# Later source numbers, a later loop for far rows and earlier block offsets in a two-layer graph kernel on one Trainium2 core

## The chip, the core and the metric

The kernel runs on one core of one Trainium2 chip. The core has five engines with a queue of instructions each: PE (TensorE, matrix products), DVE (VectorE), ACT (ScalarE), POOL (GpSimd, which here issues the indirect gathers) and SP (SyncE, which issues most other DMAs). They meet only at semaphores. The metric is the device time of one execution in microseconds (us); the lower, the better.

## The reference, cut to what matters

Two graph layers follow each other on 6250 nodes of 128 features and 100000 edges. The edges are sorted by `dst`. `src` is in no order.

```
msg = h[src] + sum_over_heads(leaky_relu(attn[rel] * (e @ fc_w.T)))     # layer 0
x   = layernorm(x + segment_sum(msg, dst))
h   = x @ W.T + b                                                       # layer 1
s1, s2 = h @ a1_w + a1_b, h @ a2_w + a2_b
e   = leaky_relu(s1[src] + s2[dst])
ex  = exp(e - segment_max(e, src)[src])
out = segment_sum((ex / segment_sum(ex, src)[src])[:, None] * h[dst], src)
x   = layernorm(x + out)
```

## The kernel before, in words

**Layer 0** is a counted loop over 196 groups of 512 edges. It also writes each edge's record (destination and place of its source within a block) into a table in DRAM (`table`, shown as `sorted_edges`) at its place in the order of the sources, so that layer 1 can go through the edges block by block. A block is 122 nodes; there are 52 blocks.

**The passage between the layers.** Thirteen chunks of four blocks (`for c in range(HCHUNKS)`) are turned on PE (L1072), normalised, and multiplied by W (L1077). DVE makes the moments (L1466, L1476) and writes the rows of h (L1471, L1480, counted by semaphore `n_hb`). Each finished chunk goes to DRAM (`h_rows`) in two DMAs: 112 partitions from SP (L543, semaphore `h_out`), 10 partitions from POOL (L659, `h_small`). The sorted records come back as two tables `tab[:, 0]` and `tab[:, 1]`, of which each place is filled in one only, so that their sum is the record. After chunk 4 DVE adds them (L1484, `tab_sum`, semaphore `t_sum`), PE turns the sum into the PSUM banks EP and AP (L1082, `t_turned`), ACT casts it (L830, L831, `t_cast`), and DVE makes from the untransposed sum `loc_i`, `loc_m` and `loc_b` (L1486 to L1488, `s_loc`): the source numbers by row. SP writes `loc_b` to `sorted_sources` in DRAM (L547) and some of `loc_i` to `near_records` (L549, `near_out`) between chunks 6 and 7. After the chunks DVE takes the two fields of the turned records apart: `sd`, the number of the row to gather (L1490, `s_dec`), and `ss` (L1491), which L1494 copies to `ssf`. Then come the scores (L1496 to L1506, `l1_ready`) and the preparation of "near" and "far" rows (L1510 to L1537), which ends with `s_trips`.

**Layer 1** has 208 steps, one for a group of 512 edges of one block. POOL gathers four times 128 rows of `h_rows` per group (`group1`, L671; `late_group1`, L679), three times where the group is "near" (every second one from the ninth on); the fourth part is then made on PE from the blocks that are in SBUF (`near_gather`, L1140) and a row of `far_rows`. There are eight buffers for groups. `group1(g)` for g of 8 or more waits for `step_done` of g - 3, which counts PE's steps. The loop for far rows runs `n_trips` times, which is once for these inputs: ACT picks the row numbers (L908), POOL gathers them (L690), SP writes them to `far_rows` (L560) and waits until that has landed. In SP's program this loop stands ahead of the loads of the source numbers of groups 4 and later (`sources`, L538); the first four are loaded ahead of it. DVE waits for these loads in `members(g + 2)` (L1544), which is a part of its step g.

DVE's step g (`step1`) is written out by hand: `update(g - 5)` (L1549 to L1554: it loads the block's offset from `blk_i` into a register, waits, and adds the sums of PE to that block), the maximum (L1587), some fifteen small operations, `members` (L1544), `spread` (L1629), and in turns `near_shift` (L1638) or `near_add` (L1646). In the last 48 steps (`TAIL`) each step ends with `early`, which finishes one block that no group will touch again: L1688 to L1703, with a wait of DVE for itself between L1702 and L1703. In the last five of them DVE also writes the final form of some blocks (`normal`, L1706).

Of the kernel before, what the change touches and what calls it, by code (L numbers as in the profile page):

```python
# [5 lines left out]
ALU = mybir.AluOpType  # L6
# [25 lines left out]
HC = 4  # L32
# [46 lines left out]
def build(nc, x, x_t, e, src_pg, dst_pg, dst_g, rel_g, fcT, attn, WT, Wn, b, a1, a1b, a2, a2b, out):  # L79
    with ExitStack() as ctx:  # L80
# [394 lines left out]
        def _(sp):  # L475
# [65 lines left out]
            for c in range(HCHUNKS):  # L541
# [3 lines left out]
                if c == HCHUNKS // 2:  # L545
                    sp.wait_ge(s_loc, 1)
                    sp.dma_start(loc_dram.rearrange("g (u r) -> (g u) r", r=P).rearrange("(c p) r -> p c r", p=P),  # L547
                                 loc_b.rearrange("p (c r) -> p c r", r=P)).then_inc(loc_out, 16)
                    sp.dma_start(near_dram.rearrange("(c a) r -> a c r", c=CH),  # L549
                                 loc_i[NEAR_PER * TG - 1:P:NEAR_PER * TG, :].rearrange("p (c r) -> p c r", r=P)).then_inc(near_out, 16)  # L550
            sp.wait_ge(loc_out, 16)
            sp.wait_ge(near_out, 16)
            for k in range(RSLOTS):
                sources(k, k, True)

# [41 lines left out]
            sp.wait_ge(h_out, 16 * HCHUNKS)  # L597
            sp.wait_ge(h_small, 16 * HCHUNKS)
# [11 lines left out]
        def _(pool):  # L610
# [46 lines left out]
            for c in range(HCHUNKS):  # L657
# [3 lines left out]
            pool.wait_ge(h_out, 16 * HCHUNKS)  # L661
            pool.wait_ge(h_small, 16 * HCHUNKS)
# [19 lines left out]
            more = group_count(pool)  # L682
            for k in range(S1):
                group1(k, k, True)
                if k == 1:
# [146 lines left out]

# [129 lines left out]
        def _(pe):  # L962
# [104 lines left out]
            for c in range(HCHUNKS):  # L1067
# [11 lines left out]
                if c == HCHUNKS // 2 - 2:  # L1079
                    pe.wait_ge(t_sum, 1)  # L1080
                    for u in range(CH):
                        mm = pe.transpose((EPS_T, AP_)[u // 4][:, u % 4 * P:(u % 4 + 1) * P],  # L1082
                                          tab_sum[:, u * P:(u + 1) * P], ident[:, :])
                    mm.then_inc(t_turned, 1)
# [87 lines left out]
        def _(dve):  # L1172
# [281 lines left out]
            for c in range(HCHUNKS + 1):  # L1454
# [27 lines left out]
                if c == HCHUNKS // 2 - 2:  # L1482
                    dve.wait_ge(s_srt, 32)
                    v.tensor_tensor(tab_sum, tab[:, 0, :], tab[:, 1, :], ALU.add).then_inc(t_sum, 1)  # L1484
                    dve.wait_ge(t_sum, 1)
                    link(v.tensor_copy(loc_i, tab_sum))  # L1486
                    link(v.tensor_scalar(loc_m, loc_i, 255, P - 1, ALU.bitwise_and, ALU.bitwise_xor))
                    v.tensor_copy(loc_b, loc_m).then_inc(s_loc, 1)  # L1488
# [319 lines left out]
```

## Time and profile before

| | |
|---|---|
| time, median of 3 runs | 2537.67 us (2537.1 to 2540.32) |
| the profiled execution: its own time | 2536.95 us |
| its span in the trace | 2535.1 us |
| busy in the span: PE, DVE, ACT, POOL | 86%, 91%, 77%, 72% |
| mean granted TensorE clock | 0.937 |
| layer 0 ends, layer 1 begins (start of the chunks, first gather) | 1496.98 us, 1541.25 us |

The span runs from the first to the last instruction of the trace; all places in the trace are given in us from its start. Busy shares are means over stages that have different limits.

### The profile page before, as it was taken

The page shows a single profiled execution, that of the slowest core. Times are in us where ns is not written, and L with a number is a line of the kernel's source. Part 1 is how long each engine was busy: PE and PEld are TensorE (multiplying, and loading weights), DVE is VectorE, ACT ScalarE, POOL GpSimd, SP SyncE. Part 2 cuts the span into 40 slices and gives each one's busy share as a digit, 9 for nine tenths or more (in the row PEclk, how much of TensorE's full clock was granted, in tenths as well). Part 3 has the DMA queues.
Part 4 walks back from the last instruction along what each step waited for, and adds up shares of the span by engine and source line. Part 5 has one row for each costly group of instructions (what it writes and reads, how often), then busy time and mean ns, then how long its engine had stood idle before and what let it go on. Part 6 is the DMA issues. An engine that isn't in the chain of part 4 may idle for free. (4 is left out here: it accounts for less than half of the span.)

```text
span 2535.1 us, 49366 instructions
## 1 busy us (share of the span) xinstructions
PE 2173.4 (86%) x12265; PEld 1562.1 (62%) x12266; DVE 2299.6 (91%) x5975; ACT 1950.8 (77%) x5574; POOL 1824.8 (72%) x1746
## 2 busy tenths in 40 slices
PE   6999999999999999999999974766667777777674
PEld 3566666666666666666666654766667666776664
DVE  9999999999999999999999986778887778888886
ACT  5788888888888888888888854777777777776666
POOL 3477777777777777777777745777777777776662
PEclk8999999999999999999999986899998888888886
DMA  4233333333333333333333324444444444443332
GB/s 139 73 101 104 104 106 101 104 103 104 105 106 102 103 103 104 105 106 101 104 102 105 105 58 98 99 100 100 98 101 99 99 100 101 98 99 86 84 82 71
DMA packets 180816, 250.92 MB, mean 99 GB/s; under 512 B 41103, under 2 KB 110172, under 8 KB 180416
## 3 DMA queue, kind: packets, MB, share of 16 engines
q1 hardware_dynamic: 125088, 145.72, 20.2%
q0 software_dynamic: 55456, 102.13, 17.1%
q8 instruction: 103, 1.69, 0.3%
q14 instruction: 169, 1.38, 0.2%
HBM read 238.37 MB, written 9.31 MB: 98 GB/s over the span
## 5 line engine op out<-in xcount | busy, mean ns | idle before, releaser
L627 POOL DMA_INDIRECT room<-in_x,pk x784 | 925.2, 1180 | 262.5 <-issue 252.5
L1010 PE MATMUL FP<-fc_sb,room 128*128 128x512 f32 x1568 | 832.4, 612 | 2.2 <-issue 2.2
L1019 PE MATMUL WP<-at_p,rel_oh 100*128 100x512 f32 x1568 | 804.2, 594 | 0.0
L671 POOL DMA_INDIRECT room<-h_rows,y x666 | 628.9, 944 | 220.5 <-issue 184.9
L754 ACT ACTIVATE w_sb<-WP 128x512 f32<-128x512 f32 x784 | 464.1, 592 | 224.9 <-PE WP L1019 219.5
L1019 PEld LDWEIGHTS WP<-at_p,rel_oh 100*128 100x128 f32 x1568 | 297.9, 190 | 376.4 <-issue 376.4
L1108 PE MATMUL FP<-ident,room 128*128 128x128 f32 x1664 | 278.2, 319 | 277.3 <-DMA room<-h_rows,y 213.9
L1359 DVE TENSOR_TENSOR z<-FP,w_sb 128x1024 f32<-128x1024 f32 x392 | 478.8, 1221 | 1.5 <-ACT w_sb L754 1.0
L1366 DVE SCALAR_TENSOR_TENSOR y<-z 128x2048 f32<-128x2048 f32 x196 | 452.2, 2307 | 0.0
L1108 PEld LDWEIGHTS FP<-ident,room 128*128 128x128 f32 x1664 | 238.0, 220 | 312.9 <-DMA room<-h_rows,y 246.0
L1010 PEld LDWEIGHTS FP<-fc_sb,room 128*128 128x128 f32 x1568 | 266.6, 190 | 43.3 <-issue 2.6
L871 ACT ACTIVATE room<-room,pr 128x129 f32<-128x129 f32 x832 | 266.6, 392 | 6.8
L852 ACT ACTIVATE accT<-accT,neg_big 128x512 f32<-128x512 bf16 x208 | 148.7, 715 | 150.6 <-DVE accT L1544 150.4
L638 POOL DMA_INDIRECT sorted_edges<-runs,spot_i x196 | 185.8, 948 | 90.4 <-issue 60.4
L761 ACT ACTIVATE boh<-arena,rank_pay 128x52 f32<-128x52 bf16 x784 | 239.7, 378 | 0.0
L1374 DVE TENSOR_TENSOR hs<-y 128x1024 f32<-128x1024 f32 x196 | 238.4, 1216 | 0.0
L1029 PEld LDWEIGHTS AP<-doh,room 128*128 128x128 f32 x1568 | 190.6, 192 | 53.5 <-DVE room L1390 53.5
L1029 PE MATMUL AP<-doh,room 128*128 128x64 f32 x1568 | 211.1, 278 | 7.1 <-DVE accT L1350 4.2
L771 ACT ACTIVATE dot<-iota_row,dloc 128x64 bf16<-128x64 f32 x784 | 206.3, 337 | 0.0
L884 ACT ACTIVATE w_sb<-boh 122x640 f32<-122x640 bf16 x100 | 73.6, 736 | 111.3 <-PE WP L1140 108.4
L878 ACT ACTIVATE boh<-w_sb,accT 122x128 bf16<-122x128 int32 x500 | 155.4, 386 | 0.0
L1587 DVE CUSTOM_DVE_ANT_0 hs<-accT,FP 128x512 f32<-128x512 f32 x208 | 142.0, 682 | 12.5 <-issue 6.0
(280 smaller groups left out, 3475.5 us busy)
## 6 DMA issues: line engine op xcount, KB each, us to landing
room<-in_e SPq DMA_DIRECT2D x196, 256.0 KB
rel_sb<-in_rel_g SPq DMA_DIRECT2D x196, 200.0 KB
z<-sorted_sources SPq DMA_DIRECT2D x208, 128.0 KB
room<-in_x,pk POOLq DMA_INDIRECT x784
room<-h_rows,y POOLq DMA_INDIRECT x666
w_sb<-far_rows SPq DMA_DIRECT2D x100, 65.0 KB
w_sb<-near_records SPq DMA_DIRECT2D x101, 61.0 KB
sorted_edges<-runs,spot_i POOLq DMA_INDIRECT x196, 2.0
```

The costliest lines, as they stand in the source:

```text
L627: pool.indirect_dma_start(xg[:, k, u, 0:P], None, x[:, :], bass.IndirectOffsetOnAxis(ap=pk[:, g, u:u + 1], axis=0)).then_inc(xg_in[k], 16)
L671: pool.indirect_dma_start(hg[k][:, u, :], None, h_dram[:, :], bass.IndirectOffsetOnAxis(ap=sd[:, g * TG + u:g * TG + u + 1], axis=0)).then ...
L754: nc.scalar.activation(w_sb[:, u // 2, u % 2, :], WP[u % 2][:, :], ACT.Copy).then_inc(w_copied, 1)
L761: ins = nc.scalar.activation(boh[:, k % 2, u, :], onehot[:, :, bass.ds(g * TG + u, 1)].rearrange("p b o -> p (b o)"), ACT.Identity, bias=0 ...
L871: nc.scalar.activation(hg[k][:, u, 0:P + 1], hg[k][:, u, 0:P + 1], ACT.Identity, bias=0.0, scale=pr[:, k % 2, u:u + 1]).then_inc(h_scaled, 1)
L1010: mm = pe.matmul(FP[u // 2][:, u % 2, :], e_sb[:, k, u, :], fc_sb[:, :], start=True, stop=True)
L1019: mm = pe.matmul(WP[u % 2][:, :], rel_oh[:, k % 2, u * P:(u + 1) * P], at_p[:, j, :], start=(j == 0), stop=(j == 1))
L1029: pe.matmul(AP_[:, 0:W], msg[:, k % 2, u, :], doh[:, k % 2, u, :], start=(u == 0), stop=False)
L1108: mm = pe.matmul(rows_of(k)[:, u * P:(u + 1) * P], hg[k][:, u, P + 1:P + 2].to_broadcast([P, P]), ident[:, :], start=True, stop=True)
L1359: v.tensor_tensor(z[:, h, :, :], FP[h][:, :, :], w_sb[:, h, :, :], ALU.mult).then_inc(z_done, 1)
L1366: v.scalar_tensor_tensor(y[:, :, :, :], z[:, :, :, :], SLOPE0, z[:, :, :, :], ALU.mult, ALU.max).then_inc(y_done, 1)
L1374: v.tensor_tensor(hs[:, :, :], y_all[:, :, 0:D4 // 2], y_all[:, :, D4 // 2:D4], ALU.add).then_inc(hs_done, 1)
```

## The change

The sum of the two tables moves behind the last chunk on DVE. PE no longer waits for it: it forms the turned sum itself, by two products with the identity that add up in PSUM, 16 matmuls in place of 8 transposes. The DMAs of the source numbers and of the near records move behind all chunks on SP, and the copy to `ssf` moves behind the scores on DVE. The last chunk's 10 partitions are written by a DMA of ACT. POOL reads the number of groups ahead of the chunks, and its part of the loop for far rows moves from behind the second group's gathers to behind the sixth's. In the last 48 steps DVE loads the next block offset right behind `spread`, and the last four offsets ahead of the last five updates.

```diff
@@ sync
                              h_sb[0:PMAIN, HC * c:HC * (c + 1), 0:HROW]).then_inc(h_out, 16)
-                if c == HCHUNKS // 2:
-                    sp.wait_ge(s_loc, 1)
-                    sp.dma_start(loc_dram.rearrange("g (u r) -> (g u) r", r=P).rearrange("(c p) r -> p c r", p=P),
-                                 loc_b.rearrange("p (c r) -> p c r", r=P)).then_inc(loc_out, 16)
...
+            sp.wait_ge(s_loc, 1)
+            sp.dma_start(loc_dram.rearrange("g (u r) -> (g u) r", r=P).rearrange("(c p) r -> p c r", p=P),
+                         loc_b.rearrange("p (c r) -> p c r", r=P)).then_inc(loc_out, 16)
+            sp.dma_start(near_dram.rearrange("(c a) r -> a c r", c=CH),
...
             sp.wait_ge(loc_out, 16)
-            sp.wait_ge(near_out, 16)
             for k in range(RSLOTS):
                 sources(k, k, True)
+            sp.wait_ge(near_out, 16)
@@ gpsimd
             pool.memset(o_all, 0.0).then_inc(o_zero, 1)
-            for c in range(HCHUNKS):
+            more = group_count(pool)
+            for c in range(HCHUNKS - 1):
                 pool.wait_ge(n_hb, HC * (c + 1))
...
-            pool.wait_ge(h_out, 16 * HCHUNKS)
-            pool.wait_ge(h_small, 16 * HCHUNKS)
+            pool.wait_ge(h_out, 16 * (HCHUNKS + 1))
+            pool.wait_ge(h_small, 16 * (HCHUNKS - 1))
...
-            more = group_count(pool)
             for k in range(S1):
+                if k == SLOTS:
+                    pool.wait_ge(s_loc, 1)
                 group1(k, k, True)
-                if k == 1:
+                if k == 5:
                     n_trips = trip_count(pool)
@@ scalar
+            act.wait_ge(n_hb, NS)
+            act.dma_start(h_blocks[PMAIN:BN, NS - HC:NS, :], h_sb[PMAIN:BN, NS - HC:NS, 0:HROW]).then_inc(h_out, 16)
@@ tensor
                 if c == HCHUNKS // 2 - 2:
-                    pe.wait_ge(t_sum, 1)
+                    pe.wait_ge(s_srt, 32)
                     for u in range(CH):
-                        mm = pe.transpose((EPS_T, AP_)[u // 4][:, u % 4 * P:(u % 4 + 1) * P],
-                                          tab_sum[:, u * P:(u + 1) * P], ident[:, :])
+                        for side_of in range(2):
+                            mm = pe.matmul((EPS_T, AP_)[u // 4][:, u % 4 * P:(u % 4 + 1) * P],
+                                           tab[:, side_of, u * P:(u + 1) * P], ident[:, :],
+                                           start=(side_of == 0), stop=(side_of == 1))
@@ vector
-                if c == HCHUNKS // 2 - 2:
-                    dve.wait_ge(s_srt, 32)
-                    v.tensor_tensor(tab_sum, tab[:, 0, :], tab[:, 1, :], ALU.add).then_inc(t_sum, 1)
...
             dve.wait_ge(t_cast, 1)
             v.tensor_scalar(sd, both, 8, None, ALU.arith_shift_right).then_inc(s_dec, 1)
+            dve.wait_ge(s_srt, 32)
+            v.tensor_tensor(tab_sum, tab[:, 0, :], tab[:, 1, :], ALU.add).then_inc(t_sum, 1)
+            dve.wait_ge(t_sum, 1)
+            link(v.tensor_copy(loc_i, tab_sum))
+            link(v.tensor_scalar(loc_m, loc_i, 255, P - 1, ALU.bitwise_and, ALU.bitwise_xor))
+            v.tensor_copy(loc_b, loc_m).then_inc(s_loc, 1)
             link(v.tensor_scalar(ss, both, 255, P - 1, ALU.bitwise_and, ALU.bitwise_xor))
             dve.wait_ge(s_loc, 1)
-            dve.wait_ge(near_out, 16)
-            v.tensor_copy(ssf, ss).then_inc(s_ssf, 1)
...
             dve.wait_ge(l1_ready, 1)
+            dve.wait_ge(near_out, 16)
+            v.tensor_copy(ssf, ss).then_inc(s_ssf, 1)
...
-            def update(g, k, lead):
-
-                r = dve.value_load(blk_i[0:1, bass.ds(g, 1)], min_val=0, max_val=NS * OROW)
+            def block_at(g):
+                return dve.value_load(blk_i[0:1, bass.ds(g, 1)], min_val=0, max_val=NS * OROW)
+
+            def update(g, k, lead, r=None):
+
+                r = block_at(g) if r is None else r
...
                 if prev:
                     spread(*prev)
+                r = block_at(g + 1 - LAG) if load_next else None
...
+            r = None
             for j in range(TAIL):
                 k = j % S1
-                step1(tail + j, k, False, k, (k - 2) % S1, j < TAIL - 2, (j + 3 < TAIL) + (j + 6 < TAIL))
+                r = step1(tail + j, k, False, k, (k - 2) % S1, j < TAIL - 2, (j + 3 < TAIL) + (j + 6 < TAIL), r=r,
+                          load_next=True)
...
+            at_last = [r] + [block_at(tail + j) for j in range(TAIL - LAG + 1, TAIL)]
             for j in range(TAIL - LAG, TAIL - 2):
-                update(tail + j, j % S1, False)
+                update(tail + j, j % S1, False, at_last[j - (TAIL - LAG)])
```

The order of instructions on DVE, at one of the last 48 steps, before (L1629 is `spread`, L1638 `near_shift`, L1694 to L1703 `early`, L1549 the load of the block offset, L1554 `update`; ISA and REGISTER_ALU rows set registers):

```order
L1629 TENSOR_TENSOR z<-WP,y 128x512
L1635 REGISTER_ALU
L1638 TENSOR_SCALAR w_sb<-w_sb 122x128 [waits w_copied,e_in1]
L1694 BN_STATS stats<-arena 122x6 [waits n_avg]
L1698 SCALAR_TENSOR_TENSOR arena<-arena,rstd 122x128 [waits n_weight]
L1702 TENSOR_SCALAR rstd<-arena 122x1 [waits st_ready]
L1703 RECIPROCAL rstd<-rstd 122x1 [waits dve_step]
L1549 REGISTER_ALU
L1549 TENSOR_LOAD blk_i
L1549 ISA x2
L1554 ISA [waits st_ready,decay_ready,step_done]
L1554 SCALAR_TENSOR_TENSOR arena<-arena,decay,FP 128x129
```

The same place in the changed kernel, whose lines have other numbers (L1551 is the load, L1560 `update`):

```order
L1635 TENSOR_TENSOR z<-WP,y 128x512
L1551 REGISTER_ALU
L1551 TENSOR_LOAD blk_i
L1551 ISA x2
L1641 REGISTER_ALU
L1644 TENSOR_SCALAR w_sb<-w_sb 122x128 [waits w_copied,e_in1]
L1702 BN_STATS stats<-arena 122x6 [waits n_avg]
L1706 SCALAR_TENSOR_TENSOR arena<-arena,rstd 122x128 [waits n_weight]
L1710 TENSOR_SCALAR rstd<-arena 122x1 [waits st_ready]
L1711 RECIPROCAL rstd<-rstd 122x1 [waits dve_step]
L1560 ISA [waits st_ready,decay_ready,step_done]
L1560 SCALAR_TENSOR_TENSOR arena<-arena,decay,FP 128x129
```

The load moved from between the reciprocal, which waits for DVE's own last result, and the update to behind `spread`. The order on POOL from the last chunks to group 8, before (L659 the chunk's DMA, L455 the number of groups, L671 the gathers, L690 the gather of far rows):

```order
L659 DMA h_rows<-arena 10x4x130 [waits n_hb] x13
L455 TENSOR_LOAD more_groups [waits s_dec,s_count,h_small,h_out]
L455 ISA x2
L671 DMA room<-h_rows,y 128x130 x8
L462 TENSOR_LOAD room [waits rel_in1]
L462 ISA x2
L687 UNCONDITIONAL_BRANCH
L687 ISA
L690 DMA w_sb<-h_rows,room 128x130 [waits rel_absd]
L687 REGISTER_ALU
L687 COMPARE_AND_BRANCH
L671 DMA room<-h_rows,y 128x130 x24
```

And in the changed kernel:

```order
L455 TENSOR_LOAD more_groups [waits s_count]
L455 ISA x2
L659 DMA h_rows<-arena 10x4x130 [waits n_hb] x12
L671 DMA room<-h_rows,y 128x130 [waits s_dec,h_small,h_out]
L671 DMA room<-h_rows,y 128x130 x15
L671 DMA room<-h_rows,y 128x130 [waits s_loc]
L671 DMA room<-h_rows,y 128x130 x7
...
L691 DMA w_sb<-h_rows,room 128x130 [waits rel_absd]
...
L671 DMA room<-h_rows,y 128x130 x8
```

Of the 32 gathers for the first eight groups 8 stood ahead of the far rows' gather, and 24 do now. On DVE the four operations on the tables stood in the middle of the chunks; now they stand behind `sd`:

```order
L1475 SCALAR_TENSOR_TENSOR arena<-FP,rstd,b_rep 122x131
L1484 SCALAR_TENSOR_TENSOR arena<-WP,rstd,b_rep 122x131 x2
L1487 TENSOR_SCALAR y<-z 128x1024 [waits t_cast]
L1489 TENSOR_TENSOR room<-w_sb 128x1024 [waits s_srt]
L1491 CAST y<-room 128x1024 [waits t_sum]
L1492 TENSOR_SCALAR w_sb<-y 128x1024 [waits dve_step]
L1493 CAST hs<-w_sb 128x1024 [waits dve_step]
L1494 TENSOR_SCALAR rank_pay<-z 128x1024
L1497 COPY s1t<-EP 52x122 [waits n_s1t,s_loc,dve_step]
```

There `sd` (L1487) is made before the tables are added (L1489), and the copy to `ssf` is no longer among these rows.

## Rows read from the trace of the kernel before

**Rows 1.** Windows: length, busy time by engine (instructions), granted clock, DMA share, GB/s.
```profile
1505.00:1509.00 4.00, 3.22 (x24) 2.52 (x22) 3.93 (x24) 2.93 (x9) 1.12 (x2) 1.00 0.36 92
1700.00:1900.00 200.00, 133.01 (x1134) 123.86 (x1133) 159.79 (x825) 153.12 (x507) 151.03 (x160) 0.96 0.45 100
2300.00:2480.00 180.00, 127.78 (x858) 117.25 (x858) 149.44 (x793) 119.26 (x395) 113.34 (x121) 0.83 0.38 83
```

**Rows 2.** Timeline of POOL: start, duration, instruction, idle time before it and its releaser.
```profile
1534.99 1.02 POOL L659 DMA_DIRECT2D h_rows<-arena  x1 [0.79 <-DVE arena L1480]
1541.25 1.04 POOL L671 DMA_INDIRECT room<-h_rows,y  x1 [5.24 <-issue]
...
1551.56 0.94 POOL L690 DMA_INDIRECT w_sb<-h_rows,room  x1 [0.42 <-issue]
...
1582.76 0.94 POOL L671 DMA_INDIRECT room<-h_rows,y  x1 [0.30 <-issue]
...
2309.34 0.94 POOL L671 DMA_INDIRECT room<-h_rows,y  x1 [1.27 <-PE AP L1129]
...
2435.79 0.94 POOL L679 DMA_INDIRECT room<-h_rows,idx  x1 [2.21 <-PE AP L1129]
```

**Rows 3.** Timeline of DVE, the last 48 steps.
```profile
2267.39 0.35 DVE L1554 SCALAR_TENSOR_TENSOR arena<-arena,decay,FP 128x129 f32 x1 [0.81 <-issue]
...
2413.66 0.16 DVE L1703 RECIPROCAL rstd<-rstd 122x1 f32<-122x1 f32 x1
2414.60 0.35 DVE L1554 SCALAR_TENSOR_TENSOR arena<-arena,decay,FP 128x129 f32 x1 [0.78 <-ACT decay L859]
...
2483.66 0.35 DVE L1554 SCALAR_TENSOR_TENSOR arena<-arena,decay,AP 128x129 f32 x1 [0.95 <-ACT decay L859]
...
2488.63 0.35 DVE L1554 SCALAR_TENSOR_TENSOR arena<-arena,decay,FP 128x129 f32 x1 [0.27 <-issue]
...
2498.51 0.34 DVE L1554 SCALAR_TENSOR_TENSOR arena<-arena,decay,FP 128x129 f32 x1
```

**Rows 4.** Line L1549 from 2413.7 to 2414.7: min/median/max ns, first and last start.
```profile
L1549 DVEq TENSOR_LOAD <-blk_i x1: 305/305/305, 2413.7 to 2413.7; - x1
L1549 DVEq FUSED_REGOPS  x1: 190/190/190, 2414.1 to 2414.1; - x1
```

**Rows 5.** Line L1549 from 1593 to 1595.
```profile
L1549 DVEq TENSOR_LOAD <-blk_i x1: 300/300/300, 1593.2 to 1593.2; - x1
```

**Rows 6.** Timeline of DVE around that load.
```profile
1593.04 0.16 DVE L1623 TENSOR_TENSOR mparts<-rest,mparts 128x1 bf16<-128x1 f32 x1
...
1594.45 0.34 DVE L1554 SCALAR_TENSOR_TENSOR arena<-arena,decay,FP 128x129 f32 x1
```

**Rows 7.** Timeline of DVE from the chunks to the third step.
```profile
1509.98 1.21 DVE L1484 TENSOR_TENSOR room<-w_sb 128x1024 f32<-128x1024 f32 x1
...
1514.11 0.89 DVE L1466 BATCH_NORM_STATS2 stats<-FP 122x6 f32<-122x128 f32 x4 [0.45 <-PE FP L1072]
...
1547.21 0.24 DVE L1537 TENSOR_SCALAR room<-room 128x1 int32<-128x1 f32 x1
...
1563.24 0.68 DVE L1544 TENSOR_TENSOR accT<-z,WP 128x512 bf16<-128x512 bf16 x1
```

**Rows 8.** Timeline of PE.
```profile
1508.28 0.61 PE L1077 MATMUL WP<-wt_sb,accT 128*122 128x131 f32 x4
...
1548.23 2.07 PE L1108 MATMUL FP<-ident,room 128*128 128x128 f32 x8 [1.45 <-DMA room<-h_rows,y]
...
1592.90 1.16 PE L1108 MATMUL FP<-ident,room 128*128 128x128 f32 x8 [0.83 <-DMA room<-h_rows,y]
```

**Rows 9.** Timeline of ACT at the end of the chunks.
```profile
1533.69 1.50 ACT L822 ACTIVATE arena<-FP,nmr,rstd 122x128 f32<-122x128 f32 x4 [0.49 <-DVE nmr L1461]
```

**Rows 10.** Time from issue to landing: SP's last chunk; then POOL's last two.
```profile
DMA to landing us min/median/max: 3.6/3.6/3.6
...
DMA to landing us min/median/max: 2.7/3.8/4.9
```

**Rows 11.** Timeline of SP behind the far rows.
```profile
1558.76 1.29 SPq L538 DMA_DIRECT2D z<-sorted_sources  x3
```

More of the change, by code:

```diff
@@ L544, in _ @@
                              h_sb[0:PMAIN, HC * c:HC * (c + 1), 0:HROW]).then_inc(h_out, 16)
-                if c == HCHUNKS // 2:
-                    sp.wait_ge(s_loc, 1)
-                    sp.dma_start(loc_dram.rearrange("g (u r) -> (g u) r", r=P).rearrange("(c p) r -> p c r", p=P),
-                                 loc_b.rearrange("p (c r) -> p c r", r=P)).then_inc(loc_out, 16)
-                    sp.dma_start(near_dram.rearrange("(c a) r -> a c r", c=CH),
-                                 loc_i[NEAR_PER * TG - 1:P:NEAR_PER * TG, :].rearrange("p (c r) -> p c r", r=P)).then_inc(near_out, 16)
+            sp.wait_ge(s_loc, 1)
+            sp.dma_start(loc_dram.rearrange("g (u r) -> (g u) r", r=P).rearrange("(c p) r -> p c r", p=P),
+                         loc_b.rearrange("p (c r) -> p c r", r=P)).then_inc(loc_out, 16)
+            sp.dma_start(near_dram.rearrange("(c a) r -> a c r", c=CH),
+                         loc_i[NEAR_PER * TG - 1:P:NEAR_PER * TG, :].rearrange("p (c r) -> p c r", r=P)).then_inc(near_out, 16)
             sp.wait_ge(loc_out, 16)
-            sp.wait_ge(near_out, 16)
             for k in range(RSLOTS):
                 sources(k, k, True)
+            sp.wait_ge(near_out, 16)
             n_trips = trip_count(sp)
@@ L595, in _ @@
             sp.sem_inc(sp_turn, 1)
-            sp.wait_ge(h_out, 16 * HCHUNKS)
-            sp.wait_ge(h_small, 16 * HCHUNKS)
+            sp.wait_ge(h_out, 16 * (HCHUNKS + 1))
+            sp.wait_ge(h_small, 16 * (HCHUNKS - 1))
             for q0, q1 in CHUNKS:
@@ L1647, in near_add, with step1 @@
                                 ALU.add).then_inc(near_added, NEAR_PER)
-            def step1(g, k, lead, at, edge_at, ahead=True, near=2, near_slot=None):
+            def step1(g, k, lead, at, edge_at, ahead=True, near=2, near_slot=None, r=None, load_next=False):
                 prev = None if lead and k < 2 else (g - 2, (k - 2) % S1, lead)
                 if not (lead and k < LAG):
-                    update(g - LAG, (k - LAG) % S1, lead)
+                    update(g - LAG, (k - LAG) % S1, lead, r)
                 max_old(g, k, lead)
@@ L1674, in step1 @@
                     near_add(g + 3, (at + 3) % S1 if near_slot is None else near_slot)
+                return r
             dve.wait_ge(o_zero, 1)
@@ L1749, in _ @@
             for j in range(TAIL - 2, TAIL):
-                update(tail + j, j % S1, False)
+                update(tail + j, j % S1, False, at_last[j - (TAIL - LAG)])
             def average(q0, q1):
```

4 lines of the change are left out of this document (removed).

## Prediction

> **What bounds the kernel now.** I read the windows first, then POOL's timeline, since POOL issues what layer 1 waits for. In 200 us from the middle of layer 1 POOL is 76% busy, DVE 80% and PE 67% [rows 1]. No share looks like a bound, but POOL's 160 gathers fill the 200 us: each is 0.94 us with 0.30 us of issue behind it, and the next starts 1.25 us after the last [rows 2]. Two steps need seven gathers, 8.74 us or 4.37 us a step. From 1551.56 on the gaps stay at 0.30 us until 2309.34, where POOL first waits 1.27 us for PE's step; by 2435.79 it is 2.21 us [rows 2], once in seven gathers. So there are two stretches with two limits. Up to about 2260, POOL's gathers set the pace: what shifts their chain shifts everything behind it, and what else is saved there is worth nothing. In the last 48 steps DVE sets it. Its `update` stands at 2267.39 and, 41 steps later, at 2483.66 [rows 3]: 5.275 us a step, 0.9 us above what the gathers need.
>
> **The last 48 steps.** In these steps DVE idles 0.78 us ahead of `update` (0.77 to 1.13 in the 42 rows from 2267.39 to 2483.66). The view names a decay of ACT, but that value had been due three steps earlier, and the gap has one length whatever else happens. The queue's own rows tell it: 0.94 us lie between the starts of the reciprocal (2413.66) and of the update (2414.60) [rows 3], and in them stand the load, 0.305 us from 2413.7, and its register work, 0.19 us from 2414.1 [rows 4]. It can't start earlier, since it stands behind DVE's wait for itself. Where other work covers it the gap shrinks: 0.27 us behind two final forms (2488.63), none where that wait is missing (2498.51) [rows 3].
>
> Behind `spread` it would be covered. In layer 1's middle the queue runs ahead: a load started at 1593.2, 0.16 us after L1623, with `members` and `spread` (0.68 us each, as L1544 in [rows 7]) still to be done, and the update at 1594.45 had no gap [rows 5, 6]. The same 1.3 us of work stand ahead of it here. What stays is the update's own register step and three waits that are met. I estimate 0.30 us from reciprocal to update, so 0.64 us saved a step; the bounds are 0.50 us (load and register work alone, 0.305 + 0.19) and 0.78 us (the whole gap).
>
> - 42 steps x 0.64 = 26.9 us (21.0 to 32.8).
> - The second step, and the two with gaps near 0.27 us: together 0.8 us.
> - The last two steps had no gap; there the load now delays `early`, about 0.15 us each: -0.3 us. The four loads at the end lie under the last `spread`s and in front of a wait for PE: 0.
> - Sum: -27.4 us. A step is then 4.64 us, still above POOL's 4.37, so nearly all of it counts. PE is busy 127.8 of 180 us here, 3.75 us a step [rows 1], and stays below.
>
> The Trainium skill (DMA: Bandwidth & Descriptors, "Latency and other measured facts") gives a register load a floor of about 0.6 us. The rows above have 0.5 us and more in one, so they agree nearly; by the page's figure the 42 steps would give 25.2 us and the time would be 1.7 us longer than I forecast.
>
> **The chunks.** DVE loses the four operations there, 1509.98 to 1513.30. But PE's part grows. A matmul of this kind is two instructions in the trace (the 8 of L1108 are four matmuls), so 16 matmuls are 32 instructions, 4 x 1.16 = 4.6 us at the upper clock level and 4 x 2.07 = 8.3 us at the lower [rows 8]. PE has chunk 4's products behind it at 1508.9 [rows 8] and the window up to 1509 shows a granted clock of 1.00 [rows 1]. It no longer pauses for the sum, so I take the upper level: 1513.4, then chunk 5's transposes, and DVE's statistics at 1514.0 against 1514.11 [rows 7]. The saved 3.3 us become a wait for PE; gain 0.1 us (at the lower level a loss of 4).
>
> The same 3.3 us come back on DVE behind `sd`. `s_trips`, which ends at 1547.45 [rows 7], moves to about 1550.6, and PE's first `rows` from 1548.23 [rows 8] to there. The second `rows` then ends near 1554.7, where it ended at 1554.9, having waited for gathers before. So steps 0 and 1 stay where they are.
>
> **The first gather** comes now at 1541.25, behind POOL's last DMA (1534.99, landed 4.9 us later, 1539.9) and the load of the number of groups [rows 2, 10]. Then it needs SP's last chunk, 3.6 us from 1534.6 [rows 10], and ACT's DMA. No row shows one of those. ACT is free at 1535.1 [rows 9]; landing lies between 2.7 and 4.9 us [rows 10], and I take SP's 3.6, as it leaves at the same time. With 0.4 us for the release, gathers start at 1539.1 (1538.2 to 1540.4): 2.1 us earlier.
>
> The Trainium skill (DMA: Bandwidth & Descriptors, "Issuing engines are not separate DMA queues") speaks against this part: all issuers share the same 16 DMA engines. The slow last landing (4.9 us against 2.7) does show them sharing. By that rule only the issue would be saved, the gathers would start at 1540.4, and the whole would take 1.3 us more.
>
> **The far rows.** The later loop holds up SP. Before, the far gather stood at 1551.56, 10.3 us behind the first gather, and SP could load source numbers 4 and later from 1558.76, 7.2 us after it [rows 2, 11]. Now 16 more gathers stand ahead of it: it starts 10.3 + 16 x 1.248 = 30.3 us behind the first, at 1569.4; SP's loads follow at 1576.6 and land about 2.5 us later (2.4 to 3.6 by other DMAs). DVE's `members(4)` in its third step, at 1563.24 before [rows 7], waits until 1579.1. That is a stall of 16 us on DVE, with ACT and PE behind it. POOL doesn't see it at first, having eight buffers. It needs `step_done` 5, PE's fourth step: `members` and `spread` 1.3 us, a maximum by 1581.2, PE's rows, back and attend about 4.1 us at the lower level, 1585.3. Its ninth group starts there, at 1585.4, against 1582.76 without a wait [rows 2]: 2.7 us late. Had the loop stayed, this group would be 2.1 us early. Behind it PE needs 4.4 us a step at worst and POOL's next group 5 us, so the chain stays closed. Bounds: the first gather's -0.9 and +1.3, the landing's +-0.5, the lower clock in the chunks +4: 0.5 to 5 us, outliers to 9.
>
> **Sum.** -27.4 + 2.7 = -24.7 us. The profiled span of 2535.1 us becomes 2510.4; its execution took 1.85 us more than its span, 2512.3; and it lay 0.7 us below the median of 2537.67: **2513 us**. This case's own range is 2505 to 2520.
>
> **Rivals.**
>
> - *Another limit takes over in the last 48 steps, at about half the gain.* The gathers, PE (at a clock of 0.83 [rows 1]) and ACT come closer together at 4.64 us, and a wait between them could hold a step at 5 us. Against: layer 1's middle runs at 4.37 us with the same three engines. -13.5 + 2.7: 2527.
> - *The stall reaches the gathers in full*, if PE restarts so slowly that groups 8 to 12 each wait: the 16 us instead of 2.7: 2526. Against: five groups' worth of buffers lie between. It decides only if PE's restart takes over 5 us a step.
> - *The load is not hidden*, because behind `spread` it holds `early` back as long as it held `update`. Then only the passage counts: 2540, within 0.2%. Against: the load that ran ahead [rows 5, 6].
> - *More than forecast:* the whole gap goes (-33) and the stall is shorter: 2505 or less.
> - *Slower:* TensorE falls to 1.2 GHz for all of the last 48 steps. Its matmuls of 1.16 us take 2.07 then [rows 8]. At a mean clock of 0.83 a third of the 3.75 us is at the lower level; all of it would be about 5.3 us, and 5.6 with the near steps unevenly long. From 5.28 us a step PE decides; 46 steps x 0.35 = +16, the saving gone: 2556. Against: PE has less idle time than now, and at 4.37 us a step the clock was 0.96 [rows 1].
>
> **How the numbers follow.** Forecast 0.70; half the gain 0.10; full stall 0.05; more than forecast 0.05; not hidden 0.05; slower 0.05. Up to 2525 lie the forecast, the better case and part of the second and third; from 2504 that is 8 in 10. What can be told from no change in this kernel is about 0.2%, 5 us: faster 0.89, same 0.06, slower 0.05.
>
> **What would show it.** Right: gaps ahead of `update` near 0.15 us or none in the last 48 steps, steps of about 4.6 us, POOL's waits there mostly gone; the first gather near 1539; PE without a pause between chunks 4 and 5, with DVE waiting some 3.5 us; `members(4)` near 1579 and the ninth group's gathers near 1585. Wrong: steps still above 5 us with the load's gap gone, DVE idle before `near_shift` or `early`, or gathers that wait again and again after 1585.

## The result, and the profile after

The changed kernel takes **2512.2 us** (median of 4 runs, 2510.5 to 2513.3); the kernel before took 2538.9 us beside it (4 runs). The ratio is 0.9895, with a 95% interval of 0.9877 to 0.9912. The forecast was 2513, from a change of -24.7 us; the medians differ by 26.7 us. The profiled execution took 2512.5 us, its span 2510.6 us.

The two spans don't line up from the start. In both traces the chunks begin with PE's first transposes, at 1496.98 before and here at 1499.48, and all code ahead of that is the same. Over all 14 profiles of this study that start lies between 1496.85 and 1501.08. So everything in the passage to layer 1 is counted from it ("+") below. Timeline of PE and of DVE after the change, in the chunks:

```profile
1499.48 0.89 PE L1074 MATMUL FP<-ident,accT 128*122 128x128 f32 x3 [3.43 <-SPq L527]
...
1511.22 1.95 PE L1085 MATMUL EP<-ident,w_sb 128*128 128x128 f32 x16
1513.01 1.95 PE L1085 MATMUL AP<-ident,w_sb 128*128 128x128 f32 x16
1514.79 0.60 PE L1074 MATMUL FP<-ident,accT 128*122 128x128 f32 x4
```

```profile
1515.43 0.69 DVE L1470 BATCH_NORM_STATS2 stats<-FP 122x6 f32<-122x128 f32 x3 [2.59 <-PE FP L1074]
...
1579.48 0.69 DVE L1547 TENSOR_TENSOR accT<-z,WP 128x512 bf16<-128x512 bf16 x1 [16.07 <-DMA z<-sorted_sources]
```

PE has no pause between chunk 4 and the sum's matmuls, and these take 3.57 us (1511.22 to 1514.79) at a granted clock of 1.00. Chunk 5's statistics stand at +15.95, where they stood at +17.13 before [rows 7]. The second DVE row is `members(4)`, at +80.0 with its stall of 16 us.

ACT's new DMA, and POOL's timeline: the last of its small DMAs, the first gather, the far gather in its new place, and the ninth group's first gather:

```profile
1536.03 0.57 ACTq L834 DMA_DIRECT2D h_rows<-arena  x1
```

```profile
1534.96 0.55 POOL L659 DMA_DIRECT2D h_rows<-arena  x1 [1.84 <-DVE arena L1484]
1539.55 1.29 POOL L671 DMA_INDIRECT room<-h_rows,y  x1 [4.04 <-DMA h_rows<-arena]
...
1570.04 0.94 POOL L691 DMA_INDIRECT w_sb<-h_rows,room  x1 [0.30 <-issue]
...
1586.44 0.94 POOL L671 DMA_INDIRECT room<-h_rows,y  x1 [5.45 <-PE AP L1133]
...
2354.59 0.94 POOL L671 DMA_INDIRECT room<-h_rows,y  x1 [1.14 <-PE FP L1133]
```

The first gather stands at +40.07, against +44.27 before [rows 2]. The ninth group stands at +86.96, against +85.78, and now it is a wait for PE. The waits that POOL had in the last 48 steps, 2 us in every seventh gather [rows 2], are down to one of 1.14 us.

Timeline of DVE in the last 48 steps: the updates of step 2 and of step 43, and between them the reciprocal and the update of one step:

```profile
2272.55 0.35 DVE L1560 SCALAR_TENSOR_TENSOR arena<-arena,decay,FP 128x129 f32 x1
...
2426.65 0.16 DVE L1711 RECIPROCAL rstd<-rstd 122x1 f32<-122x1 f32 x1
2426.88 0.35 DVE L1560 SCALAR_TENSOR_TENSOR arena<-arena,decay,FP 128x129 f32 x1
...
2459.05 0.35 DVE L1560 SCALAR_TENSOR_TENSOR arena<-arena,decay,AP 128x129 f32 x1 [0.15 <-DVE nmr L1455]
```

41 steps take 186.5 us: 4.549 us a step, against 5.275 before [rows 3]. From the reciprocal to the update it is 0.23 us, against 0.94. The windows (columns as in [rows 1]) show DVE filled:

```profile
2280.00:2455.00 175.00, 129.67 (x978) 121.55 (x978) 167.97 (x885) 132.53 (x443) 131.81 (x140) 0.87 0.45 98
```

DVE is busy 168 of 175 us. The load is still there, its parts as long as they were [rows 4], but it runs while `members` and `spread` do. Line L1551 from 2425 to 2440:

```profile
L1551 DVEq TENSOR_LOAD <-blk_i x4: 302/304/313, 2424.8 to 2438.4; - x4
L1551 DVEq FUSED_REGOPS  x4: 190/190/190, 2425.1 to 2438.7; - x4
```

Behind step 47 something new stands. Timeline of DVE: its update, the last `spread`, then the first three of the five last updates; and PE's product that follows the first of them:

```profile
2476.97 0.34 DVE L1560 SCALAR_TENSOR_TENSOR arena<-arena,decay,AP 128x129 f32 x1
...
2482.15 0.69 DVE L1635 TENSOR_TENSOR hs<-WP,y 128x512 f32<-128x512 f32 x1
2485.95 0.35 DVE L1560 SCALAR_TENSOR_TENSOR arena<-arena,decay,FP 128x129 f32 x1 [3.10 <-issue]
2486.55 0.35 DVE L1560 SCALAR_TENSOR_TENSOR arena<-arena,decay,AP 128x129 f32 x1 [0.26 <-DVE arena L1560]
2488.64 0.35 DVE L1560 SCALAR_TENSOR_TENSOR arena<-arena,decay,FP 128x129 f32 x1 [1.74 <-PE FP L1133]
```

```profile
2486.44 2.06 PE L1133 MATMUL FP<-room,z 128*128 128x129 f32 x8 [5.06 <-DVE arena L1560]
```

Four loads in one block hold the first update 3.10 us, and PE's product waits for exactly this update.

The difference of the spans, stretch by stretch:

| stretch | before | after | difference |
|---|---|---|---|
| up to the chunks (same code) | 1496.98 | 1499.48 | +2.50 |
| chunks to the ninth group's gathers | 85.78 | 86.96 | +1.18 |
| ninth group to step 0 of the last 48 (its update at 2258.30 and 2264.62) | 675.54 | 678.18 | +2.64 |
| step 0 to step 47 (2502.01 and 2476.97) | 243.71 | 212.35 | -31.36 |
| step 47 to the end | 33.09 | 33.63 | +0.54 |
| span | 2535.1 | 2510.6 | -24.5 |

The third stretch has POOL without a pause in both, but for one of 1.19 us; in the 14 profiles it lies between 674.2 and 678.8 us, whatever the kernel. It and the first are scatter, some 5 us of it, and the change's own parts are the other three rows. They add up to -29.6 us, 3 us more than the medians differ, so they scatter too; the averages behind the next table show by how much.

### The profile page after: what moved, and what is told of

It is laid out like the page before. It is cut to its first block, busy times and chain, and to the rows that moved or that the text cites. A ratio compares the mean times of both kernels' runs of the same rounds, so it can differ in the third digit from the quotient of the medians.

```text
span 2510.6 us, 49414 instructions
## 1 busy us (share of the span) xinstructions
PE 2152.7 (86%) x12289; PEld 1544.8 (62%) x12290; DVE 2299.5 (92%) x5975; ACT 1950.2 (78%) x5574; POOL 1826.2 (73%) x1745
## 4 chain that ended last, share of the span: by engine, by line
DVE 40%; issue 25%; POOL 15%; PE 8%; DVEq 6%; DMA 6%; ACT 0%; SPq 0%; POOLq 0%; ACTq 0%
DVE y L1370 17%; POOL room L671 15%; DVE hs L1378 10%; DMA room<-h_rows,y 5%; DVEq L1350 4%; DVE room L1394 4%; PE FP L1112 3%; PE AP L1133 2%; DVE accT L1354 2%; DVE z L1363 1%; PE FP L1133 1%; DVE joh L1344 1%; DVE room L1386 1%; DVE arena L1215 0%; DVEq L1551 0%
## 5 line engine op out<-in xcount | busy, mean ns | idle before, releaser
L671 POOL DMA_INDIRECT room<-h_rows,y x666 | 630.2, 946 | 213.6 <-issue 180.7
L1031 PE MATMUL AP<-doh,room 128*128 128x64 f32 x1568 | 212.2, 278 | 7.1 <-DVE accT L1354 4.2
L1547 DVE TENSOR_TENSOR accT<-z,WP 128x512 bf16<-128x512 bf16 x208 | 141.4, 680 | 17.1 <-DMA z<-sorted_sources 16.1
```

The costliest lines, as they stand in the source:

```text
L671: pool.indirect_dma_start(hg[k][:, u, :], None, h_dram[:, :], bass.IndirectOffsetOnAxis(ap=sd[:, g * TG + u:g * TG + u + 1], axis=0)).then ...
L1031: pe.matmul(AP_[:, 0:W], msg[:, k % 2, u, :], doh[:, k % 2, u, :], start=(u == 0), stop=False)
```

## The experiments

All results in one table; the columns behind the ratio are read from the profiles: first gather and ninth group behind the chunks' start, whether POOL waits for the ninth group, step 0 to 47, and step 47 to the end.

| kernel | median us | ratio to before (95%) | first gather | ninth group | 0 to 47 | 47 to end |
|---|---|---|---|---|---|---|
| before | 2538.3 to 2539.0 | | +44.27 | +85.78 | 243.7 | 33.1 |
| changed | 2512.2 | 0.9895 (0.9877, 0.9912) | +40.07 | +86.96, waits | 212.4 | 33.6 |
| tail_only | 2510.1 | 0.9891 (0.9876, 0.9906) | +43.36 | +84.89 | 214.3 | 35.3 |
| passage_only | 2537.3 | 0.9996 (0.9987, 1.0005) | +39.49 | +86.97, waits | 242.9 | 31.4 |
| loop_at_fourth | 2505.5 | 0.9870 (0.9854, 0.9885) | +39.63 | +81.50 | 212.2 | 34.6 |
| loop_at_second | 2512.5 | 0.9901 (0.9886, 0.9917) | +39.64 | +88.29 | 212.7 | 34.7 |
| eight_rows | 2506.6 | 0.9872 (0.9856, 0.9887) | +39.96 | +81.78 | 212.5 | 33.9 |
| no_act_dma | 2512.8 | 0.9897 (0.9882, 0.9912) | +40.65 | +87.98, waits | 215.4 | 34.0 |
| double_load | 2532.8 | 0.9978 (0.9969, 0.9987) | +39.90 | +86.88, waits | 236.1 | 34.3 |
| end_unbatched | 2503.6 | 0.9859 (0.9844, 0.9874) | +40.13 | +81.81 | 212.3 | 31.9 |
| the same again | 2503.7 | 0.9861 (0.9846, 0.9876) | +39.93 | +81.76 | 213.5 | 32.0 |
| load_ahead_of_members | 2540.8 | 1.0007 (0.9998, 1.0016) | +40.06 | +87.12, waits | 243.8 | 34.1 |
| sources_held | 2510.1 | 0.9889 (0.9874, 0.9904) | +42.02 | +85.42 | 214.4 | 35.0 |
| sum_in_chunks | 2506.1 | 0.9871 (0.9856, 0.9886) | +41.75 | +83.52 | 214.8 | 32.7 |

The last two columns scatter by some 3 us and 2 us among kernels whose code there is the same. In the ten profiles with one early load a step behind `spread`, steps 0 to 47 take 212.2 to 215.4 us, 213.4 on average; the two with the load in `update` average 243.3. The end takes 33.6 to 35.3 us (34.4 on average) in the nine profiles that load four offsets in one block, and 31.4 to 33.1 (32.2) in the five that don't. By these averages the last 48 steps give 29.9 us, the block at the end costs 2.2 and the passage 1.2: 26.5 us together, as the medians have it (26.7).

### The two halves of the change

**tail_only** is the kernel before with `block_at`, `load_next` and `at_last` of the diff, and nothing else.

> The kernel before with the early block offsets alone. Theory A (what the two traces give when laid side by side: the tail is worth 31.4 us between the updates of steps 0 and 47, the four loads in one block at the end cost 0.5 us): 30 to 32 us below the kernel before, some 2508 us, steps of the last 48 near 4.5 us. Rival B (the terms on record): 27.4 us below, 2511 us. Rival C (part of the 31 us is not the load's but comes from the new phase in which the last 48 steps are entered): steps fall by less than 0.7 us, 25 us or less in all.

Measured: 28.3 us below the kernel before. Steps 0 to 47 fall by 29.4 us in a trace in which nothing ahead of them was changed. From step 2 to step 43 (2267.15 to 2455.17) a step is 4.586 us, 0.69 less than before; sources_held, whose last 48 steps have the same code, gives 4.541, 0.73 less. Rival C's 25 us are out, though a part of 2 to 3 us by the way in which the last 48 steps are entered can't be told from scatter. A and B lie 3 us apart, and the total stands between them, below A's 30 to 32; the trace says why: 29.4 us are won in the steps and 2.2 us lost behind them.

**passage_only** is the changed kernel with the offset loaded in `update` again.

> The changed kernel with the block offsets loaded in the update again; all that the change does around layer 1's start stays. Theory A (the changed trace: chunks to ninth group 1.2 us longer, then one pause of POOL of 1.2 us; the 2.5 us by which its chunks start later lie ahead of all that is changed and are scatter): 1 to 4 us above the kernel before, gathers first 40 us behind the first transposes of the chunks, members(4) 80 us behind them. Rival B (the term on record): 2.7 us above. Rival C (the 2.5 us are the change's too): 5 to 7 us above.

Measured: 2537.3 us, 1 us below the kernel before, and the interval of the ratio holds 1. C is out. With the early offsets on both sides the passage costs 2.2 us by the medians (2512.2 against 2510.1), where the intervals of the two ratios overlap. The passage as a whole is worth nothing that can be told from zero, though it holds a gain of 4 us at the first gather and a wait of 5 us at the ninth group.

### Where the loop for far rows stands

```
             for k in range(S1):
                 ...
                 group1(k, k, True)
-                if k == 5:
+                if k == 3:        # loop_at_second: k == 1
                     n_trips = trip_count(pool)
```

> The changed kernel with the loop for far rows behind the fourth group's gathers instead of the sixth's. Theory A (SP's loads of source numbers 4 and later wait for that loop and hold DVE, ACT and PE; the far column is picked 15.9 us after the first gather, so behind the fourth group, 20 us after it, POOL need not wait for it): the far gather comes 10 us earlier, members(4) near 69.7 us instead of 80.0 behind the chunks' first transposes, the ninth group's gathers without a wait of POOL (before them 5.45 us, of which 0.3 is issue): 4 to 5.5 us below the changed kernel, some 2507.5 us. Rival (the ninth group waits for PE whatever the loop does): same as the changed kernel, 2512.

> The changed kernel with the loop for far rows behind the second group's gathers, where it stood before. Theory A (the loop had to move because the sum was moved: the far column is picked 15.9 us after the first gather, the second group ends 10 us after it): POOL stands some 6 us with six groups of gathers still to issue, members(4) comes 14 us earlier than in the changed kernel but the ninth group starts at about the same time: within 2 us of the changed kernel, 2512 to 2514. Rival (what the prediction says, that with the loop left this group would be 2.1 us early): the stall of 2.7 us and 2.1 us more are won, 2507.5.

Behind the fourth group: 2505.5 us, 6.8 us below the changed kernel, more than A's 4 to 5.5; in the trace the ninth group comes 5.5 us sooner, and the rest is within the scatter. The interval of its ratio overlaps that of the changed kernel by a little, and just misses that of loop_at_second, which takes as long as the changed one. POOL's timeline has the far gather without a wait, and no pause at the ninth group:

```profile
1557.12 0.94 POOL L691 DMA_INDIRECT w_sb<-h_rows,room  x1 [0.30 <-issue]
...
1578.35 0.97 POOL L671 DMA_INDIRECT room<-h_rows,y  x1 [0.30 <-issue]
```

DVE's stall ahead of `members(4)` is 5.34 us there, at +69.6 (1566.48 against a start at 1496.85), and costs nothing any more. Behind the second group POOL stands:

```profile
1554.37 0.94 POOL L691 DMA_INDIRECT w_sb<-h_rows,room  x1 [7.18 <-ACT room L910]
```

ACT picks the far column only at 1553.37, since DVE's chain to `s_trips` is late by the sum that was moved behind it. The 7.18 us stand in front of 24 gathers and reach the ninth group in full, +88.29. The kernel is as fast as the changed one, as A said. So the loop had to leave its place once the sum was moved, but went two groups too far.

### Is it only SP's loads behind the loop?

**eight_rows** gives the rows of source numbers 4 to 7 four buffers of their own, loaded ahead of the loop; the loop stays behind the sixth group.

```
+            for k in range(RSLOTS):
+                sp.dma_start(more_row[:, k, :],
+                             loc_dram[RSLOTS + k:RSLOTS + k + 1, :].to_broadcast([P, GE])).then_inc(more_in[k], 16)
```

> The changed kernel, its loop for far rows behind the sixth group as it is, but with eight buffers for the first rows of source numbers, so that SP loads numbers 0 to 7 ahead of that loop. Theory A (the stall of 16 us and the ninth group's wait come from SP's loads of numbers 4 to 7 behind the loop, and from nothing else that the loop does): no wait of DVE ahead of members(4), the ninth group's gathers 81.5 us behind the chunks' first transposes and without a wait, as in the kernel with the loop behind the fourth group: 2505 to 2508 us. Rival (POOL's far gather in its later place costs by itself, or the eighth group's near row is then late): a wait of the same length one to four steps later, 2510 us or more.

Measured: 2506.6 us, the ninth group at +81.78 without a wait. But DVE's stall is not gone. Its timeline (line numbers of this kernel) has `members(4)` without one, and then `near_shift` with one:

```profile
1562.74 0.68 DVE L1560 TENSOR_TENSOR accT<-accT,WP 128x512 bf16<-128x512 bf16 x1
...
1579.45 0.23 DVE L1657 TENSOR_SCALAR w_sb<-w_sb 122x128 int32<-122x128 int32 x1 [12.51 <-DMA w_sb<-near_records]
```

SP loads the record of `near_shift` behind the loop too. The rival had the later wait right and its price wrong. By then PE has done the steps that the ninth group needs, and the buffers of gathers take up a stall of 12.5 us whole. What cost was a stall of 16 us one step sooner, ahead of `step_done` 5.

### What brought the first gather forward

**no_act_dma** lets POOL send the last chunk's small rows again; **sources_held** is tail_only with one line more, SP's first loads of source numbers held until those rows have landed.

```
             sp.wait_ge(near_out, 16)
+            sp.wait_ge(h_small, 16 * HCHUNKS)
             for k in range(RSLOTS):
                 sources(k, k, True)
```

> The changed kernel with the last chunk's small rows sent by POOL again, as before; POOL's early load of the number of groups stays. Theory A (the first gather waits for the last small landing; POOL's issue of it stands 1.5 us behind where ACT's stands now, and it landed 4.9 us after issue against 3.5 us by ACT): first gather 42.5 to 43 us behind the chunks' first transposes instead of 40.1, and all that follows 2.5 us later: 2514 to 2515 us. Rival (all issuers share the same DMA engines, so only the issue itself is saved): 0.5 to 1.5 us later, 2513 us.

> The kernel with the early block offsets alone, and SP holding its first four loads of source numbers (128 KB each) until the last small rows of the chunks have landed. Theory A (before the change these loads leave at the same time as the last chunk's rows and slow their landing; that they come later is most of why the changed kernel's first gather is early): the last small landing 3.3 to 3.9 us behind its issue instead of 4.9, the first gather 42.0 to 42.8 us behind the chunks' first transposes instead of 43.4, the total 0.5 to 1.5 us less, 2509 us, which the total alone can hardly tell. Rival (the landing is slow by POOL's own issue, 1.02 us in the kernel before): first gather as it was, 43.4.

Without ACT's DMA the first gather comes at +40.65, 0.6 us later, and the median is 0.6 us up: the rival's number, not A's. POOL's own last DMA isn't slow there; its gather follows 3.85 us behind the issue:

```profile
1535.58 0.55 POOL L659 DMA_DIRECT2D h_rows<-arena  x1 [0.79 <-DVE arena L1483]
1539.43 1.29 POOL L671 DMA_INDIRECT room<-h_rows,y  x1 [3.31 <-DMA h_rows<-arena]
```

In the kernels whose `sources` leave together with the last chunk's rows it is 6.2 us. POOL's timeline in tail_only, where SP's four loads of 128 KB go out at 1536.47:

```profile
1536.31 1.01 POOL L659 DMA_DIRECT2D h_rows<-arena  x1 [0.79 <-DVE arena L1480]
1542.54 1.04 POOL L671 DMA_INDIRECT room<-h_rows,y  x1 [5.21 <-issue]
```

And with these loads held back and nothing else changed, POOL's timeline in sources_held:

```profile
1536.31 1.02 POOL L660 DMA_DIRECT2D h_rows<-arena  x1 [0.78 <-DVE arena L1481]
1540.64 1.24 POOL L672 DMA_INDIRECT room<-h_rows,y  x1 [3.32 <-issue]
```

The issue is as long (1.02 us), the wait behind it 1.9 us shorter. So the loads of the source numbers had slowed the landing. From the chunks' start the gather comes 1.3 us sooner (+42.02 against +43.36), since POOL's issue itself stands 0.6 us later there. The total, 2510.1 us, can't tell 1.9 us, as expected.

The Trainium skill ("DMA: Bandwidth & Descriptors", "Issuing engines are not separate DMA queues") says that DMAs of several issuers run on the same engines and that starting them from several engines saves only the issue. Both runs agree: 0.6 us for the other issuer, 1.9 us for taking SP's traffic out of the way.

**sum_in_chunks** puts the sum of the tables back, with ACT's DMA, POOL's early load, the unbatched end (below), and the loop behind the third group.

> The kernel with the end unbatched, but the sum of the tables back in the chunks on DVE with its eight transposes on PE, and SP's writes of the source numbers in their old place; ACT's DMA and POOL's early load stay, and the loop for far rows stands behind the third group, where the far column is then ready. Theory A (moving the sum gives 1.2 us in the chunks, and some 1.3 us by keeping SP's loads off the last landing): first gather 42 to 43 us behind the chunks' first transposes, no wait of POOL at the ninth group, 83.5 to 84.5 us instead of 81.8: 2 us above the kernel with the end unbatched. Rival (the move gives nothing once the loop stands right): within 0.7 us of it.

Measured on the chip of the second run of end_unbatched: 2506.1 against 2503.7 us, first gather +41.75 against +39.93, ninth group +83.52 against +81.76. By the trace the move of the sum is worth 1.8 us where the loop stands right, near A's 2 (its first gather was to come at +42 or later), and the rival's 0.7 is out; the intervals of the two ratios overlap. SP's loads leave 0.4 us behind ACT's DMA there, at 1539.08 and 1538.66, and the first gather follows that DMA 4.17 us later instead of 3.52.

### What hides the load

**double_load** loads each early offset twice; **load_ahead_of_members** loads it once, 1.2 us sooner:

```
                 max_out(g, k, lead, at)
+                r = block_at(g + 1 - LAG) if load_next else None
                 if ahead:
                     members(g + 2, (k + 2) % S1, lead and k < S1 - 2)
                 if prev:
                     spread(*prev)
-                r = block_at(g + 1 - LAG) if load_next else None
```

> The changed kernel with every early block offset of the last 48 steps loaded twice in a row, the first of the two unused. Theory A (behind spread a load costs nothing, since the engine still has work queued): the second is hidden in part too, some 0.3 us a step by the load and its register work, up to 14 us: 2512 to 2526 us. Rival (the load was never hidden, and the gap went because the wait on itself had stood in front of it): 0.5 us or more a step, 24 us and more, 2536 us or above.

> The changed kernel with the early block offset of the last 48 steps loaded 1.2 us sooner in each step, ahead of members instead of behind spread. It is as early for its update, but DVE has just waited for itself there and has nothing long queued. Theory A (a load takes some 0.7 us of the engine's queue, and what hides it is the 0.69 us operations queued in front of it; doubled behind spread it cost 0.45 us a step): a gap of 0.4 to 0.7 us ahead of members in every step, steps of 5.0 to 5.2 us, 2530 to 2540 us. Rival (it is enough that the load stands well ahead of its update): no gap, 2512 us.

Ahead of `members` the load wins nothing: 2540.8 us, the steps from 0 to 47 take 243.8 us as in the kernel before. Its timeline of DVE:

```profile
2434.27 0.16 DVE L1629 TENSOR_TENSOR mparts<-rest,mparts 128x1 bf16<-128x1 f32 x1
2434.98 0.69 DVE L1547 TENSOR_TENSOR accT<-z,WP 128x512 bf16<-128x512 bf16 x1 [0.55 <-issue]
```

The gap has moved from `update` to `members`: 0.55 to 0.65 us, 0.60 on average (19.8 us in 33 rows from 2280 to 2455), of the 0.67 us a step that are lost again. What makes up the rest no row names. Steps of 5.21 us and the total lie just above A's 5.2 and 2540. The rival is out: being early is not enough.

The second load behind `spread` costs 0.5 us a step (236.1 against 212.4 us for 47), 20.6 us in the median. That is more than A allowed and less than the rival. Line L1551 has the two loads of one pair 0.7 us apart:

```profile
L1551 DVEq TENSOR_LOAD <-blk_i x2: 301/302/304, 2432.0 to 2432.7; - x2
```

So a load takes 0.7 us of DVE's queue. One of them behind `spread` leaves DVE busy 96% of the time, and of the second only 0.2 us are hidden. The cover is real, and one load uses nearly all of it.

### The four loads at the end

```
-            at_last = [r] + [block_at(tail + j) for j in range(TAIL - LAG + 1, TAIL)]
             for j in range(TAIL - LAG, TAIL - 2):
-                update(tail + j, j % S1, False, at_last[j - (TAIL - LAG)])
+                update(tail + j, j % S1, False, r if j == TAIL - LAG else None)
```

> The kernel with the loop behind the fourth group, and in addition the four loads in one block at the end taken apart again: the first of the five last updates goes ahead with the offset that it already has, the other four load theirs in place. Theory A (that block holds the first of the five updates 3.1 us where it had been held 0.9 us, and PE's next product waits for this update, 5.3 us idle against 2.8): some 2 to 3 us below the kernel with the loop behind the fourth group, 2502.5 to 2503.5 us. Rival (the term on record: the four loads lie in front of a wait for PE and cost nothing): 2505.5 us.

> The kernel with the loop behind the fourth group and the end unbatched once more, on the chip of the kernels beside it, to compare them with it: 2503.5 us, within 1 us.

Measured: 2503.6 and 2503.7 us, 1.8 us below loop_at_fourth; the intervals of the two ratios overlap, so the trace has to carry it. Timeline of DVE in end_unbatched, and PE's product:

```profile
2477.38 0.34 DVE L1560 SCALAR_TENSOR_TENSOR arena<-arena,decay,FP 128x129 f32 x1
2478.80 0.35 DVE L1560 SCALAR_TENSOR_TENSOR arena<-arena,decay,AP 128x129 f32 x1 [1.08 <-issue]
2480.07 0.35 DVE L1560 SCALAR_TENSOR_TENSOR arena<-arena,decay,FP 128x129 f32 x1 [0.92 <-PE FP L1133]
```

```profile
2477.86 2.06 PE L1133 MATMUL FP<-room,z 128*128 128x129 f32 x8 [1.86 <-DVE arena L1560]
```

PE waits 1.86 us for that update instead of 5.06 (5.04 in loop_at_fourth), and step 47 to the end takes 31.9 and 32.0 us instead of 34.6. This kernel has the lowest median of all, 8.6 us below the changed one.

## Why the prediction was right, and where it was not

The time, the sign and the chief cause were right; the sizes of most terms were off and partly cancelled.

**The last 48 steps, -27.4.** The mechanism held: the load was what the gap was made of, it is hidden behind `spread`, POOL's waits went, and no other limit took over. The gain a step was 0.69 us (tail_only) and 0.73 us (changed kernel) instead of 0.64: from the reciprocal to the update 0.23 us are left and not the estimated 0.30. Steps 0 to 47 gave 29.4 us (tail_only) and 31.4 us (changed kernel), 29.9 by the averages of the profiles. The weak point of the argument was that the row of layer 1's middle [rows 5, 6] showed that a load *can* be hidden, not how much cover there was. load_ahead_of_members and double_load show how close it was: 1.2 us sooner, or a second load, and nearly all of it is gone.

**"The four loads at the end ... : 0".** This step failed. They do lie in front of a wait for PE, but PE itself was waiting for the update behind them. From step 47's update to PE's product it is 7.27 us before (2502.01 to 2509.28), 9.47 us now and 6.29 us with the loads apart: 2.2 us lost, and 1.0 us that was to be had. The gain in the steps, 2.5 us above the forecast, and this loss of 2.2 us cancel, and that is why the term of -27.4 came out.

**The chunks, 0.1.** The matmuls took 3.57 us and not 4.6, so the gain was 1.2 us. The row of [rows 8] gave the time of a burst of eight with its end in it, 0.145 us each; the rows above overlap (16 take 1.95 us, the next 16 start after 1.79), and in the run of 32 each adds 0.11 us.

**The first gather, 2.1 us earlier.** It was 4.2. 1.2 us of it are the chunks. ACT's DMA, on which the text spent its estimate, is worth 0.6 us. What was overlooked is in SP's part of the diff: `sources` behind the last chunk no longer runs beside the last landing, 1.9 us in sources_held. The slow landing of 4.9 us in [rows 10] was the sign of it: the prediction took it for sharing, and didn't ask what it shared with. The last 0.5 us fit POOL's earlier load of the number of groups (from POOL's issue to the gather 4.33 us in sources_held, 3.85 in no_act_dma), but that edit wasn't run alone, so this share is argued and not shown.

**The far rows, +2.7 for the ninth group.** The chain was right link by link: `members(4)` was to stall 16 us and did (16.07), at +80.0 instead of +82.1, which is the first gather's 2.1 us. From there to the ninth group 6.3 us were forecast and 6.96 came. In all +1.2 us instead of +2.7.

**"Had the loop stayed, this group would be 2.1 us early".** Wrong. It would have been later, +88.29, since the prediction moved `s_trips` by 3.3 us in one paragraph and didn't carry that to the far column in the next: ACT picked it 3.3 us behind `s_trips` before (1550.55 against 1547.21) and does so still, so POOL, with its gathers sooner, stands waiting for it. Just behind the fourth group both waits are gone.

**The rivals.** Half the gain, a load that isn't hidden, the stall in full, and TensorE's clock: none occurred. Of "more than forecast" the half on the gap came near, 0.69 to 0.73 of its 0.78 us; the time did not. The mean granted clock in the last 48 steps was 0.87, against 0.83 [rows 1], so some of the time at the lower of its two levels, as before. The scatter of the stretches that the change doesn't touch (2.5 and 2.6 us in the first pair of traces) is as large as the errors above. The forecast was also taken from a median of 2537.67, where the kernel before took 2538.9 beside the changed one: -24.7 us were forecast and -26.7 measured. So the closeness of 2513 to 2512.2 is partly luck.

## What to carry to other kernels

In this kernel a register load cost its engine's queue, not only its consumer: put such a load behind the longest queued operations, look at how much of that cover one load uses, and never gather several of them in front of an operation for which another engine waits. When work is moved later in one engine's chain, carry the new time to everything picked, loaded or looped behind it, and place a blocking loop at the first point where its input is ready: here two groups earlier were worth 5.5 us by the trace and 6.8 by the medians, about a fifth of the main gain. Look at a transfer's landing together with what leaves beside it, whoever issues it: here 0.2 us behind it.

## What the runs showed of the hardware

- A load of a register from SBUF on DVE has a row of 0.30 us and 0.19 us of register work, but two of them in a row start 0.7 us apart (double_load). Exposed, it showed as a gap of 0.78 us ahead of an update, 0.55 to 0.65 us ahead of `members`, and four in a block as 3.10 us; the first of these four has a row of 0.98 us (at 2482.3 in the changed kernel), which nothing here explains.
- DVE's queue ran nearly two operations of 0.69 us ahead of its execution where no wait on itself stood in between (the load at 2424.8, while `members` ran from 2424.62 and `spread`, which stands ahead of the load, started only at 2425.22). The Trainium skill ("Advanced Engine Details and Errata", "Engine Queue Depths") gives VectorE a queue of eight on trn2. No run here came near filling it, so they neither bear out nor speak against that number.
- Four loads of 128 KB that SP started 0.2 us behind POOL's small DMA made the first gather, which waits for that DMA's landing, 1.9 us later (6.23 against 4.33 us from POOL's issue). Which engine issued the small one made 0.6 us.
- Fp32 matmuls of 128x128 in a run of 32 instructions took 3.57 us at the upper clock level (granted clock 1.00), 0.11 us each.
